# Scaling the softmax shifts of even units on VectorE instead of ScalarE, in an attention and gate kernel

## The reference, cut to what matters

```python
xn = _layernorm(x)
q, k, v = proj(Wq, bq), proj(Wk, bk), proj(Wv, bv)      # 16 heads of 32
scores = einsum('bhid,bhjd->bhij', q, k) / sqrt(32)
im = arange(L) % 256
scores = where(im[:, None] >= im[None, :], scores, -1e30)
probs = softmax(scores, axis=-1)
out = einsum('bhij,bhjd->bhid', probs, v) @ Wo.T + bo
y = clip((xn @ sign(W).T) * scale + bias, -100, 100)    # sign: +1 or -1
return x + out * silu(y)
```

## Time and profile before

| what | value |
|---|---|
| median of three runs | 1672.88 us (1670.03 to 1674.52) |
| the profiled execution | 1672.39 us, of which the span of the trace 1670.6 us |
| TensorE busy | 1602.0 us, 96% |
| VectorE busy | 1184.2 us, 71%, 1790 instructions |
| ScalarE busy | 1195.6 us, 72%, 3057 instructions |
| GpSimd busy | 1239.8 us, 74%, 1223 instructions |
| mean granted clock of TensorE | 0.995 of full speed |

### The profile page before, as it was taken

One profiled execution on the slowest core, in us unless ns is written; L12 is line 12 of the kernel. 1 busy time (PEld: TensorE's weight loads), 2 busy tenths in 40 slices (PEclk: granted clock), 3 DMA queues, 4 the chain that ended last, 5 costly groups with the idle time before them and its releaser, 6 DMA issues.

```text
span 1670.6 us, 34222 instructions
## 1 busy us (share of the span) xinstructions
PE 1602.0 (96%) x11931; PEld 685.3 (41%) x11931; DVE 1184.2 (71%) x1790; ACT 1195.6 (72%) x3057; POOL 1239.8 (74%) x1223
## 2 busy tenths in 40 slices
PE   9988999989999899998999999999999989999988
PEld 4333344434444344443444434443344434444433
DVE  7787776787667766686767866678676776667762
ACT  3476787777777777687776787866787777777762
POOL 0277767887788779887688776798768897678865
PEclk9999999999999999999999999999999999999999
DMA  7323312333224422243122532233312322222121
GB/s 214 118 36 74 89 41 64 96 85 76 52 65 98 91 56 52 79 112 79 46 58 71 126 70 49 61 86 101 86 41 63 99 77 63 52 58 71 44 66 51
DMA packets 182951, 125.97 MB, mean 75 GB/s; under 512 B 104734, under 2 KB 157214, under 8 KB 182332
## 3 DMA queue, kind: packets, MB, share of 16 engines
q1 hardware_dynamic: 182300, 123.40, 29.6%
q10 hardware_dynamic: 480, 0.39, 0.1%
HBM read 41.40 MB, written 17.02 MB: 35 GB/s over the span
## 4 chain that ended last, share of the span: by engine, by line
PE 77%; ACT 6%; issue 6%; POOL 4%; DVE 3%; SPq 3%; DMA 1%; POOLq 0%; ACTq 0%; DVEq 0%
PE pJ L576 30%; PE pO L820 13%; PE pJ L801 10%; PE pS L774 3%; PE pJ L797 3%; PE pJ L671 3%; PE pJ L675 3%; PE pJ L672 3%; POOL acc L1311 2%; SPq L1415 2%; PE pS L756 2%; PE pJ L740 2%; ACT pS L940 2%; ACT PT L920 2%; PE pS L757 1%
## 5 line engine op out<-in xcount | busy, mean ns | idle before, releaser
L1311 POOL TENSOR_TENSOR acc<-acc,PT 128x512 f32<-128x512 f32 (+1 forms) x714 | 874.7, 1262 | 15.8 <-PE pO L820 10.8
L920 ACT ACTIVATE PT<-pJ 128x512 f32<-128x512 f32 (+1 forms) x1080 | 614.7, 583 | 328.8 <-PE pJ L801 313.2
L801 PE MATMUL pJ<-QK 97*128 97x512 f16 (+3 forms) x1280 | 384.5, 318 | 5.5 <-ACT acc L920 3.4
L1172 DVE TENSOR_REDUCE mx<-pS 128x3 f32<-128x1536 f32 (+3 forms) x264 | 377.4, 1440 | 0.0
L1156 DVE TENSOR_REDUCE mx<-pS 128x1 f32<-128x384 f32 (+3 forms) x330 | 209.0, 636 | 139.9 <-PE pS L757 138.0
L1168 DVE TENSOR_REDUCE mx<-pJ 128x1 f32<-128x512 f32 (+3 forms) x264 | 151.7, 585 | 180.0 <-PE pJ L774 117.5
L820 PE MATMUL pO<-PT,V 128*32 128x512 f32 (+2 forms) x2800 | 259.4, 484 | 1.1 <-ACT PT L920 1.1
L940 ACT ACTIVATE pS<-pS,a 128x128 f32<-128x128 f32 (+1 forms) x480 | 251.3, 527 | 1.2
L797 PE MATMUL pJ<-QK 128*128 128x128 f16 x1024 | 180.6, 221 | 13.3 <-ACT PT L920 10.0
L576 PE MATMUL pJ<-xT,wh_k 128*128 128x512 f16 x512 | 192.5, 378 | 0.0
L576 PE MATMUL pJ<-wh_v,xT 128*128 128x512 f16 x512 | 189.9, 379 | 1.4 <-ACT acc L920 1.3
(11 more groups left out here) (177 smaller groups left out, 2681.8 us busy)
## 6 DMA issues: line engine op xcount, KB each, us to landing
QK<-sg SPq DMA_DIRECT2D x762, 64.0 KB, 2.0
xs<-in_x SPq DMA_DIRECT2D x60, 256.0 KB, 3.2
xr<-in_x SPq DMA_DIRECT2D x58, 256.0 KB, 3.1
out<-xr SPq DMA_DIRECT2D x58, 256.0 KB, 2.5
QK<-aT SPq DMA_DIRECT2D x256, 1.0 KB, 1.7
QK<-in_x SPq DMA_DIRECT2D x8, 256.0 KB, 4.0
rq<-moved SPq DMA_DIRECT2D x120, 2.0 KB, 1.8
QK<-in_mqk SPq DMA_DIRECT2D x2, 512.0 KB, 10.0
```

Of the source, the lines that this page charges most:

```text
L801: ins = e.matmul(slot[:, to:to + 512 - q0], k4[0:97, j, kc], q4[0:97, j, q0:512], start=True, stop=True)
L920: e.activation(probabilities_at(i), bank("t", i)[:, 0:cols], ACT.Exp, scale=SS).then_inc(s_p, 1)
L1172: e.tensor_reduce(mx[:, par, part, :].rearrange("p (j q) -> p j q", q=4)[:, 0:3, qi], pS[:, :, c0:c0 + w], AX.X, ALU.max).then_inc(s_m0, 1)
L1311: e.tensor_tensor(a, a, PT[:, RING_AT[i] % NPT, 0:width * len(heads)].rearrange("p (j q) -> p j q", j=len(heads)), ALU.add).then_inc(s_ap, 1)
```

## The change

The copy on ScalarE (step 3) is taken out of `sum_rows`. In its place VectorE issues a `tensor_scalar` that multiplies the same 4, 2 or 1 values by `-SS`, from `mx` to `a16`, 0.005 behind the maximum in the order of times, which means directly behind it in VectorE's list. It waits for the maximum in front of it (`s_mc`), for the transposition that reads the previous contents of `a16` (`s_aT`), and for the last exponentials that used them (`s_e`). The exponentials wait for `s_ac` as before, which VectorE now signals. Nothing else is moved.

```diff
             def sum_rows():
                 for i, (n, qi, width, heads) in enumerate(C_TILES):
                     par = n // 2 % 2
-                    c = slice(4 * heads[0] + qi, 4 * heads[-1] + qi + 1, 4)
-                    yield at_c(i) + TM["ex"][0]
-                    ln.wait_ge(s_mc, i + 1)
-                    ln.wait_ge(s_k, 3)
-                    if n > 1:
-                        ln.wait_ge(s_aT, n - 1)
-                    if n - 2 in C_LAST:
-                        ln.wait_ge(s_e, C_LAST[n - 2] + 1)
-                    e.activation(a16[:, 0, c], mx[:, 0, 0, c], ACT.Copy, scale=-SS).then_inc(s_ac, 1)
                     yield at_c(i) + TM["ex"][1]
                     ln.wait_ge(s_ac, i + 1)
...
             def row_maxima():
                 for i, (m, qi, width, heads) in enumerate(C_TILES):
                     yield at_c(i) + TM["mx"][2]
+                    c = slice(4 * heads[0] + qi, 4 * heads[-1] + qi + 1, 4)
                     ln.wait_ge(s_C, i + 1)
...
-                    e.tensor_reduce(mx[:, 0, 0, 4 * heads[0] + qi:4 * heads[-1] + qi + 1:4],
+                    e.tensor_reduce(mx[:, 0, 0, c],
                                     pS[:, S_BANK["c", i], 0:width * len(heads)].rearrange("p (j k) -> p j k", j=len(heads)),
                                     AX.X, ALU.max).then_inc(s_mc, 1)
+                    yield at_c(i) + TM["mx"][2] + 0.005
+                    ln.wait_ge(s_mc, i + 1)
+                    ln.wait_ge(s_aT, m - 1)
+                    if m - 2 in C_LAST:
+                        ln.wait_ge(s_e, C_LAST[m - 2] + 1)
+                    e.tensor_scalar(a16[:, 0, c], mx[:, 0, 0, c], -SS, None, ALU.mult).then_inc(s_ac, 1)
```

## The result

| | before | changed |
|---|---|---|
| median | 1673.81 us (5 runs, 1670.03 to 1674.52) | 1682.28 us (5 runs, 1679.79 to 1686.60) |
| ratio | | 1.0054, 95% interval 1.0041 to 1.0067 |
| span of the profiled execution | 1670.6 us | 1678.0 us |

The change made the kernel 0.54% slower, 9 us. The forecast was 1690 us (+17 us) in a range of 1668 to 1707; the rival "only even counts held" had 1683. So the measured time lies in the range, but it is the rival's and not the forecast's.

What follows compares the result with a forecast made beforehand. TensorE, busy 96% of the span, was taken as the bound, so gains must come from its gaps. Terms -3 + 18.2 + 2 = +17 us on the median 1672.88 us gave 1690 us, range 1668 to 1707 us.

Steps and rivals of the forecast that it cites:

- only even counts held: Rival, chance 0.20: in the row-score stretches GpSimd delays only scalings of two or four values; +10 us, 1683 us.
- ScalarE's side: Row-score stretches: ScalarE loses 330 small copies, so TensorE waits less for exponentials; -3 us, bounds 0 and -16.
- VectorE's side, without neighbours: 330 added scalings, 0.2 us each on VectorE, mostly absorbed by idle time; four places pass the slack, +1.1 us in all.
- Beside GpSimd: Deciding term: VectorE's scalings wait for GpSimd's running instruction on the shared port pair, stalling TensorE in the stretches; +18.2 us.
- the leading case: Likeliest case, chance 0.45: scalings of one, two and four values all wait for GpSimd; forecast 1690 us.
- the full hold: All 330 scalings, single values included, wait for GpSimd, 87 us in total; costs +18.2 us, chance 0.45.
- the same walk: Waits carried through all 30 stretches' trace rows, largest TensorE excess taken once each; +18.2 us, or +12.4 without single values.
- lateness that grows: Rival, chance 0.05: late exponentials hold ScalarE's queue and the probabilities in all 30 stretches by 1.5 us; 45 us, 1715 us.
- Further work on GpSimd's side: GpSimd's additions wait up to 0.1 us for a scaling, on the chain in seven stretches; 0 to 4 us, taken as +2.
- What the profile was to show: Signs: scalings' mean about 0.43 us if held, 0.17 flat if not; ScalarE's busy time down 80 us; TensorE waits of 1 to 2 us.
- The other side: Rival, chance 0.08: nothing held, ScalarE bounds seven gappy stretches, so removing copies pays; -7 to -16 us, about 1662 us.

## Why the prediction was right and wrong

**ScalarE's side, -3 us.** Not shown by itself. One value per instruction has all of the relief and all of VectorE's added list, and its ratio to before is 0.9999 (0.9990 to 1.0007); the two terms, -3 and +1.1 us, would make 0.9989. So either the relief is smaller or the list costs more than the sum had, or a larger relief and a larger cost cancel. The stretch from 760 us (unit 30) did as said: its length did not change, though its exponentials no longer had copies between them.

**VectorE's side, without neighbours, +1.1 us.** Small, but not confirmed in size. With one value each the 30 stretches grew by 3.3 us, and with the 240 single ones alone the kernel is 2 us slower; ScalarE's relief is in both.

**Beside GpSimd.** The mechanism was right: place, price of single waits, order of the units, and the sum of waiting (36 us expected for the even counts, 44 measured; 87 and 88 for all). The step that failed is the one that took the 240 of one value in: the leading case had them held, in the term of +18.2 us. I had no row of a one-element operation; the smallest one that I had seen held had two elements. I gave the full hold 0.45 against 0.20 for the even counts alone. The 240 instructions show that one value is not held: 95 chances, none taken, and the term is 12.4 us by the same walk.

I had read the 240 into the Trainium skill's rule (SBUF — State Buffer, "Who interferes with whom") by the condition on counts to which it refers (VectorE: DVE Perf Modes, "Mode 2×_2P — use both read ports for one tensor"). That condition speaks of the outermost dimension of more than one element, "even (or odd and equal for src and dst)", and does not say what becomes of an operand that has no such dimension; that one element is taken in was my reading, and the runs are against it. The rule's other part, that the one who starts first keeps the ports to its end, agrees with the 0.03 us between the two ends.

**The terms.** For the even counts the sum was -3 + 12.4 + 1 = +10 us; measured +9. For all counts it was +17; two values in every single scaling measured +18 by the ratio and +20 by the medians. That these sums agree so well is in part luck, for the places do not. The stretches of units 12, 20, ... 60 were named as the costly ones, 13.1 of the 18.2 us of the full hold, but in the changed kernel they grew by 5.8 us, and half of that is there without a hold. A reason that would fit, not tested: the walk kept TensorE fixed, and every stall of TensorE gives VectorE time to catch up. Units 4, 8, 40 and 56 made up for it with 3.7 us. The path was another one, too. I had followed VectorE's lateness to the bank that `L1203` frees, and its wait is 0.3 us in the changed kernel; what grew were TensorE's waits for the chunks' exponentials, by 4.3 us, which the prediction had as a cause of its own only in the rival "lateness that grows". Further work on GpSimd's side, +1 to +2 us, is not to be seen: `L1309` has 1255 ns on average (1262 before).

**What the profile was to show.** Mean 0.43 us for all scalings held; it is 0.29, with two kinds and no tail in one of them, which is the sign that told. ScalarE's busy time was to fall by 80 us and fell by 30: I had used the sum of durations there, although the prediction itself counts 0.09 us each.

**The other side.** ScalarE's relief paying 7 to 16 us had 0.08. With one value each, where no hold stands against it, it does not appear in the time.

**What stays open.** The relief alone (the copies left out with nothing in their place), and VectorE's list alone (the scalings into an unread tile), were not measured, so how the level result splits into two terms is not shown. Nor was a scaling of three values measured: what is shown is that one is free and two and four are held, and not whether "more than one" or "even" is the rule. None of the kernels beats the one before; the one with one value per instruction equals it.

## What to carry to other kernels

Before moving a small SBUF-to-SBUF operation to VectorE, look at what GpSimd does at that moment: its price may be the rest of GpSimd's current instruction and sometimes the next one too, here 0.6 us on average over the 72 held for an operation of 0.17 us, and everything behind it in VectorE's list can pay. Where such an operation has only a few elements, issue them one by one (shown here for `tensor_scalar` with one value each), and compare instructions of one line by shape, because a mean over shapes hides that one kind is never held. To price such a move, walk the trace's own rows with each wait put in; that gave the waiting within a fifth and the time within 1 to 3 us once the right instructions were counted, but not the places where the time was lost.

## What the runs showed of the hardware

A `tensor_scalar` from SBUF to SBUF with one element per partition was never held by GpSimd: 0 of 95 in the changed kernel, 0 of 296 with one value per instruction and 0 of 99 with the 240 alone. With two or four elements it was held each time that it started inside a GpSimd instruction with more than 0.17 us to go, 68 of 68 in the changed kernel and 157 of 157 with two values in every single one, and ended 0.03 us after a GpSimd instruction. Two elements that were one read twice in the source were held like two different ones (92 of the 240 took more than 0.2 us). The kind of GpSimd's instruction made no difference: those 157 ran beside five kinds (`L1313`, `L1321`, `L1336`, `L1338`, `L1350` of that kernel). Independent one-element operations start 0.07 us apart, so four of them cost 0.34 us, beside 0.17 us for one of four with nothing in its way, and 0.75 us for one of four on average in the changed kernel.
